# A transformer layer on 8 cores: earlier second half of the value weights, and the value bias on another engine

## The reference

```python
xn = layernorm(x)
q, k, v = split(xn @ W_attn + b_attn)            # 16 heads of 64
att = q k^T / 8 / temperature + slope_h * (kpos - qpos), causal
y = softmax(att) @ v @ W_proj + b_proj
g, u = xn @ wg^T / 127, xn @ wu^T / 127          # int32 weights, 3072 wide
out = x + y + (silu(g) * u) @ wd^T / 127
```

## Time and profile before

| | |
|---|---|
| Median of 3 runs | 975.07 us |
| The profiled execution | 976.52 us |
| its span, core 0 (the slowest) | 975.0 us |
| spans of cores 1 to 7 | 969.2, 968.2, 967.1, 970.6, 966.0, 964.9, 972.8 us |
| PE busy | 906.5 us (93%) |
| DVE, ACT, POOL busy | 500.9, 482.1, 285.3 us |
| Chain that ended last, by engine | PE 82%, DMA 6%, DVE 5%, issue 5%, ACT 2% |
| Mean DMA rate | 173 GB/s |

### The profile page before, as it was taken

One profiled execution on the slowest core, in us unless ns is written; L12 is line 12 of the kernel. 1 busy time (PEld: TensorE's weight loads), 2 busy tenths in 40 slices (PEclk: granted clock), 3 DMA queues, 4 the chain that ended last, 5 costly groups with the idle time before them and its releaser, 6 DMA issues.

```text
span 975.0 us, 19076 instructions; the slowest of 8 cores (964.9 to 975.0 us)
## 1 busy us (share of the span) xinstructions
PE 906.5 (93%) x6274; PEld 407.9 (42%) x6274; DVE 500.9 (51%) x1113; ACT 482.1 (49%) x583; POOL 285.3 (29%) x305
## 2 busy tenths in 40 slices
PE   2899899999999999999999999999983999999998
PEld 1445334444444444444444444444431444444443
DVE  4632377777777777777777777777210011110111
ACT  1545477776777767777767767766444000000000
POOL 2010123343333333233333333344470042412200
PEclk9999999999999999999999999999995999999999
DMA  8826089999999999999999999899579967342211
GB/s 186 197 71 109 9 163 202 230 213 209 164 204 206 221 208 194 196 203 197 198 214 206 184 188 198 185 207 213 119 186 186 240 189 257 128 176 85 87 44 44
DMA packets 334100, 168.56 MB, mean 173 GB/s; under 512 B 305459, under 2 KB 317748, under 8 KB 333108
## 3 DMA queue, kind: packets, MB, share of 16 engines
q1 hardware_dynamic: 325648, 136.88, 69.8%
q0 software_dynamic: 5328, 22.02, 11.4%
q10 hardware_dynamic: 3028, 8.44, 2.2%
HBM read 84.46 MB, written 20.97 MB: 108 GB/s over the span
## 4 chain that ended last, share of the span: by engine, by line
PE 82%; DMA 6%; DVE 5%; issue 5%; ACT 2%; DVEq 0%; ACTq 0%; SPq 0%
PE ps_gu L728 29%; PE ps_dn L847 17%; PE ps_m L708 10%; PE ps_s L792 8%; PE ps_y L805 6%; PE ps_dn L841 6%; PE ps_s L761 5%; DMA h_sc<-hst 3%; DMA xstage<-xin 2%; DVE sc L549 2%; DVE hst L492 1%; DMA bv_s<-battn_v 1%; ACT pr L665 1%; PE ps_y L708 1%; DVE st L502 0%
## 5 line engine op out<-in xcount | busy, mean ns | idle before, releaser
L665 ACT ACTIVATE pr<-sc,cm 128x2048 bf16<-128x2048 f32 (+15 forms) x256 | 291.0, 1198 | 60.0 <-DVE cm L549 59.9
L549 DVE CUSTOM_DVE_ANT_0 sc<-ps_s,ramp 128x1024 f32<-128x1024 f32 (+7 forms) x256 | 243.8, 988 | 74.6 <-PE ps_s L792 65.4
L728 PE MATMUL ps_gu<-xnT,wubuf 128*128 128x512 bf16 x768 | 206.0, 382 | 29.9 <-DVE hst L492 29.8
L728 PE MATMUL ps_gu<-xnT,wgbuf 128*128 128x512 bf16 x768 | 205.8, 382 | 6.1 <-ACT gh_s L619 6.1
L847 PE MATMUL ps_dn<-wdres,hb 128*128 128x512 bf16 x768 | 168.6, 380 | 0.0
L407 POOL TENSOR_SCALAR th_s<-th_s 128x512 f32<-128x512 f32 x96 | 59.4, 619 | 256.3 <-ACT th_s L617 256.1
L549 DVE CUSTOM_DVE_ANT_0 sc<-ps_s,ramp,cm 128x1024 f32<-128x1024 f32 (+7 forms) x128 | 100.0, 816 | 56.3 <-PE ps_s L792 55.4
L590 DVE SCALAR_TENSOR_TENSOR outsb<-ps_dn,xres 128x512 f32<-128x512 f32 x32 | 20.7, 687 | 200.8 <-PE ps_dn L847 149.6
L413 POOL TENSOR_TENSOR gs_s<-th_s,gh_s 128x512 bf16<-128x512 f32 x96 | 111.3, 1159 | 26.7 <-POOL th_s L407 25.9
L728 PEld LDWEIGHTS ps_gu<-xnT,wubuf 128*128 128x128 bf16 x768 | 66.8, 98 | 113.1 <-issue 54.5
L708 PE MATMUL ps_m<-xnT,wqk_b 128*128 128x512 bf16 x480 | 114.0, 380 | 0.0
(11 more groups left out here) (56 smaller groups left out, 455.7 us busy)
## 6 DMA issues: line engine op xcount, KB each, us to landing
h_sc<-hst SPq DMA_DIRECT2D x96, 128.0 KB, 3.2
hb<-h_sc SPq DMA_DIRECT2D x4, 3072.0 KB, 16.7
stg_i<-wg_r SPq DMA_DIRECT2D x20, 512.0 KB, 4.8
stg_i<-wu_r SPq DMA_DIRECT2D x20, 512.0 KB, 5.2
xstage<-xin SPq DMA_DIRECT2D x16, 512.0 KB, 6.8
xres<-xin POOLq DMA_DIRECT2D x16, 512.0 KB, 5.4
out<-outsb ACTq DMA_DIRECT2D x15, 512.0 KB, 2.7
stg_f<-wqk_r SPq DMA_DIRECT2D x12, 512.0 KB, 5.6
```

The costliest lines, as they stand in the source:

```text
L549: e.tensor_tensor_reduce(scores(n, g + (2 if b == 2 else 0), c0, w), ps_s[:, g * 1024:g * 1024 + w], ramp[:, T - wide + c0:T - wide + c0 + ...
L665: e.activation(pr[n % 3][:, b0 * 128:(b0 + blocks) * 128], scores(n, r, 0, blocks * 128), AF.Exp, bias=cm[:, at:at + 1], scale=-1.0).then_ ...
L728: mm = e.matmul(ps_gu[:, up * 512:up * 512 + 512], w[:, w0:w0 + 128], xnT[:, dc * T + tb * 512:dc * T + tb * 512 + 512], start=(dc == 0), ...
```

## The change

Two parts. In the start, POOL issues both halves of `wv_b` (and the Q and K weights between them) at once; the values of the second half are made up for at PE's i = 4 instead of 8, behind Q and K of the first 512 tokens, and from i = 5 on both halves are made for each tile. DVE's `evac_q` moves from its turns 7, 11, 15 to 6, 10, 14. In the rest, the value bias moves from ACT, after its last gate, to POOL: one pair each at batches k = 69, 93, ..., 189, two more behind `silu(90)`; and the 12 loads of down weights and the one of projection weights are issued together behind these two, no longer spread over six `silu`.

```diff
-        v_at = {i: [(i - 1, 0)] for i in range(1, 9)}
-        v_at[8] += [(tt, 1) for tt in range(4)]
-        for i in range(9, NT + 1):
+        v_at = {i: [(i - 1, 0)] for i in range(1, 5)}
+        v_at[4] += [(tt, 1) for tt in range(4)]
+        for i in range(5, NT + 1):
             v_at[i] = [(i - 1, 0), (i - 1, 1)]
-        v_at[9] += [(4, 1), (5, 1)]
-        v_at[10] += [(6, 1), (7, 1)]
...
 # gpsimd
-            e.dma_start(out=wv_b[:, 0:4096], in_=wv_r[0, :, :]).then_inc(sem["l_wv0"], 16)
-            cast_qk(0)
-            e.wait_ge(sem["l_const"], 16 * 5)
-            e.tensor_scalar(bv_s[:, :], bv_s[:, :], 127.0, None, AluOpType.mult).then_inc(sem["g_bv"], 1)
+            for half in range(2):
+                e.dma_start(out=wv_b[:, half * 4096:(half + 1) * 4096], in_=wv_r[half, :, :]).then_inc(
+                    sem[f"l_wv{half}"], 16)
+                if half == 0:
+                    cast_qk(0)
...
-            e.wait_ge(sem["v_xn"], 4)
-            e.dma_start(out=wv_b[:, 4096:8192], in_=wv_r[1, :, :]).then_inc(sem["l_wv1"], 16)
...
+            def value_bias(p):
+                e.wait_ge(sem[f"l_yt{p % 2}"], 16 * (p // 2 + 1))
+                if p == 0:
+                    ...   # bv_s times 127, once
+                e.tensor_scalar(VY[:, p * VS:p * VS + T], VY[:, p * VS:p * VS + T], bv_s[:, p:p + 1], None,
+                                AluOpType.add).then_inc(sem["g_y"], 1)
+            def late_weights():
+                ...       # the same waits as before
+                for j in range(HCP):
                     cast_down(j)
+                e.dma_start(out=wpj_b[:, :], in_=wproj_r[:, :]).then_inc(sem["l_wp"], 16)
             for k in range(NST):
                 for f in groups_ended(k, 0):
                     gate_and_loads(f)
+                if k % 24 == 21 and k >= 48:
+                    value_bias(k // 24 - 2)
             for f in range(NF_ATT + 1, NF):
                 gate_and_loads(f)
-                if NF_ATT + 2 <= f < NF_ATT + 2 + HCP // 2:
-                    late_weights(f - NF_ATT - 2)
+                if f == NF_ATT + 2:
+                    value_bias(NHP - 2)
+                    value_bias(NHP - 1)
+                    late_weights()
 # vector
-                if i >= 7 and i % 4 == 3:
+                if i >= 6 and i % 4 == 2:
                     evac_q(i // 4 - 1)
 # scalar
-            e.wait_ge(sem["g_bv"], 1)
-            for p in range(NHP):
-                e.wait_ge(sem[f"l_yt{p % 2}"], 16 * (p // 2 + 1))
-                e.activation(VY[:, p * VS:p * VS + T], VY[:, p * VS:p * VS + T], AF.Identity,
-                             bias=bv_s[:, p:p + 1]).then_inc(sem["a_y"], 1)
 # tensor
-                    if i == 8 and x == 1:
+                    if i == 4 and x == 1:
+                        ...   # Q and K of tokens 0 to 511, from behind the values of i = 4
                         e.wait_ge(sem["l_wv1"], 16)
...
-            e.wait_ge(sem["a_y"], NHP)
+            e.wait_ge(sem["g_y"], NHP)
```

More of the change, by code:

```diff
@@ L39 @@
     "l_hb0", "l_hb1", "l_yt0", "l_yt1", "l_xr0", "l_xr1", "l_xr2", "l_xr3", "s_out0", "s_out1",
-    "g_set", "g_w", "g_bv", "g_th", "g_s", "g_xr",
+    "g_set", "g_w", "g_bv", "g_y", "g_th", "g_s", "g_xr",
     "v_t", "v_cbq", "v_ln", "v_xn", "v_q", "v_mx", "v_rc", "v_y", "v_h", "v_out",
-    "a_c", "a_sd", "a_xe", "a_v", "a_k", "a_e", "a_th", "a_g", "a_y",
+    "a_c", "a_sd", "a_xe", "a_v", "a_k", "a_e", "a_th", "a_g",
     "p_c", "p_xT", "p_v", "p_qk", "p_s", "p_av", "p_g", "p_u", "p_d", "p_dl",
@@ L437, in cast_down @@
                     sem[f"l_wd{j // 2}"], 16)
[L439 to L449, removed]
+            def value_bias(p):
+                e.wait_ge(sem[f"l_yt{p % 2}"], 16 * (p // 2 + 1))
+                if p == 0:
+                    e.wait_ge(sem["l_const"], 16 * 5)
+                    e.tensor_scalar(bv_s[:, :], bv_s[:, :], 127.0, None, AluOpType.mult).then_inc(
+                        sem["g_bv"], 1)
+                    e.wait_ge(sem["g_bv"], 1)
+                e.tensor_scalar(VY[:, p * VS:p * VS + T], VY[:, p * VS:p * VS + T], bv_s[:, p:p + 1], None,
+                                AluOpType.add).then_inc(sem["g_y"], 1)
+            def late_weights():
+                e.wait_ge(sem["p_qk"], 8 * NHP)
+                e.wait_ge(sem["v_mx"], 2 * NSB)
+                e.wait_ge(sem["a_e"], 4 * NU)
+                for x in "abs":
+                    for i in range(3):
+                        e.wait_ge(sem[f"l_t{x}{i}"], 16 * ((NU - 1 - i) // 3 + 1))
+                for j in range(HCP):
                     cast_down(j)
-                if 2 * part + 2 == HCP:
-                    e.dma_start(out=wpj_b[:, :], in_=wproj_r[:, :]).then_inc(sem["l_wp"], 16)
+                e.dma_start(out=wpj_b[:, :], in_=wproj_r[:, :]).then_inc(sem["l_wp"], 16)
             for k in range(NST):
@@ L754, in _ @@
                         e.wait_ge(sem["l_wv0"], 16)
-                    if i == 8 and x == 1:
+                    if i == 4 and x == 1:
+                        e.wait_ge(sem["a_xe"], 4)
+                        e.wait_ge(sem["l_wq0"], 16)
+                        e.wait_ge(sem["a_c"], 1)
+                        q_or_k(0, 0, ps_m, range(DC)).then_inc(sem["p_qk"], 1)
+                        q_or_k(0, 1, ps_y, range(DC)).then_inc(sem["p_qk"], 1)
                         e.wait_ge(sem["l_wv1"], 16)
@@ L765, in _ @@
                     mm.then_inc(sem["p_v"], 1)
[L766 to L771, removed]
                 if i >= 9 and i % 4 == 1:
```

## The result

The changed kernel takes 985.77 us (median of 4 runs, 983.83 to 987.71), the kernel before 974.97 (4 runs, 973.22 to 976.52): a ratio of 1.0116, 95% interval 1.0097 to 1.0135. It is slower by 10.8 us, where I had forecast 978.0 and a range up to 982.0. The sign was right, the size was not.

A forecast was written before the change was run, and what follows sets the result against it. PE, 82% of the chain, was taken as the bound, so only its idle or slow-clock places counted. 976.5 - 3.4 + 5.0 + 0.5 - 0.7 = 977.9, taken as 978.0 us; range 973.5 to 982.0.

The forecast's parts named there:

- Tile loads that now share engines with it (tile 7) are wanted later than before: At the start, claimed that tile loads sharing DMA engines with the early wv_b half are wanted later; no cost was added.
- Until 36.17 us PE has done the same work: At the start, claimed PE's work is the same in both kernels up to 36.17 us.
- 0.6 us, while POOL has nothing else due: At the start, issuing wv_b's second half sooner costs POOL one issue of 0.6 us, with nothing else due there.
- The wait for `wv_b` behind K: At 36.17 us PE waits for wv_b's second half behind Q and K: +0.8 us, bounds 0 and 2.9.
- The gain of 3.4 for PE's order: At the start: tile 7's wait goes (-2.7), core 0's clock fall goes (-1.5), a wv_b wait comes (+0.8): -3.4 us.
- evac_q: One turn earlier, DVE normalises tiles 10 and 14 late and PE idles: 2 x 2.5 = +5.0 us, bounds 0 and 8.0.
- the rival: The clock falls behind both evac_q waits, at tiles 10 and 14: +3.0 us, 981.0 in all; chance 0.11.
- The bias pass: Value bias on POOL during attention: 2.3 us per 128x2048 pass, costing +0.5 us, bounds 0 and 6 x 2.5.
- The cover by 19.44 us: At the gates' end, 12 us of POOL work before silu(91) is swallowed by PE's 19.44 us idle: cost 0.
- The loads together (-0.7): Down weights 4.6 us later let group 91's store land sooner before the projection: -0.7 us, bounds -4.9 and +2.8.
- The port lock: Rival: in attention, each of six POOL bias passes holds DVE up for 2.3 us, 984.9 in all; chance 0.04.
- the start's first term: Second half of wv_b queued early with catch-up at i = 4: a net gain, -3.4 us.

The follow-up runs named there:

- se_catchup: Kernel before with only PE's new order at the start (catch-up at i = 4, two values per tile from i = 5): 973.90 us, ratio 0.9995.
- wv_early: Kernel before with only the second half of wv_b issued early, right behind the Q and K weights: 976.08 us, ratio 1.0010.
- s_evac_back: Kernel before with all edits of the start except evac_q, which stays in DVE's turns 7, 11, 15: 979.46 us, ratio 1.0046.
- v_only: Kernel before with the start unchanged and only the rest changed (value bias on POOL, 13 late weight loads together): 974.88 us, ratio 1.0005.
- two_op: Changed kernel with POOL's value bias pass written as two operations, add the bias and multiply by 1.0: 985.75 us, ratio 1.0121 to the kernel before.
- se_iota_late: Kernel before with PE's new order and wv_b's second half queued at once; evac_q and the ramp as before: 974.91 us, ratio 1.0018.

## Why the prediction was wrong

By its own sum, the start was to cost -3.4 + 5.0 = +1.6 us. It costs 10.5 at the start of attention: PE's order -0.7, the two edits beside the first tiles +5.0, evac_q +6.1.

- **"Tile loads that now share engines with it (tile 7) are wanted later than before": this step failed.** I looked at tile 7 and not at tiles 4 and 5, the next ones due. Tile 5's statistics stand before tile 4's normalising in DVE's order, and tile 4 is what PE needs ahead of Q and K. "Until 36.17 us PE has done the same work" was wrong with it: PE comes to tile 4's transpose at 30.55 on core 0 before, and at 35.52 in the changed kernel, having waited 3.84 us for it.
- **A moved wait was not priced at all.** The edit took POOL's wait for the constants away from in front of the ramp. I costed the issue that came in ("0.6 us, while POOL has nothing else due") and not the iota that now runs while DVE normalises tile 0. The two failures make each other worse: at the start of attention 0.7 and 1.5 us alone, 5.0 together; in the mean span 2.7, 1.2 and 5.9.
- **The wait for `wv_b` behind K: right as a place, hidden by the failure.** Predicted 0.8 (0 to 2.9). In the changed kernel there is none: the half lands at 10.43 + 23.9 = 34.3 us and PE comes to it at 42.4. Where PE comes in time and the load is issued late it is 1.1 in the mean and 2.7 at most (se_catchup). The gain of 3.4 for PE's order was 0.7: the 2.7 for tile 7 and the 1.5 of clock were core 0's, the slowest, and over the eight cores the wait for tile 7 was 0 to 2.66 us, 1.2 in the mean, with a fall behind it on core 0 alone.
- **evac_q: mechanism, place and sign right, size 6.1 for 5.0.** Two idles of 2.00 us each against 2.15 foreseen, ended by DVE's xn_st as foreseen. What is missing is the fall of the clock behind one of the two (1.7 us), which stood in the rival and in the bounds (up to 8.0), not in the value. Comparing 2.15 with a 2.06 behind which the clock held was a poor guide: behind 2.00 us it fell at one of the two tiles and held at the other, and it also held behind 2.50 (wv_early, core 1) and 2.87 (s_evac_back, core 1).
- **The bias pass: 5.45 us for 2.3, and no cost.** I took it from casts and a two-operation pass; neither row has one operation. The term of +0.5 was 0.
- **The cover by 19.44 us held**, though silu(91) started 17.7 us behind the end of silu(90) and not 12: PE idled 13.51 us before up group 92 and 1.01 before 95. **The loads together (-0.7)** measured nothing, v_only is at 1.0005; beside the start with `evac_q` back, loads and value bias cost 3.4 us, by a cause that stays open. The wait for `wpj_b` came (0.5 to 4.7 us, some with a clock fall); from the last score to the projection it is 107.0 us in the mean of the changed kernel's cores, 105.5 in two_op and 105.6 before.
- **The port lock** had 0.04 as a rival in attention, and there it did nothing: 687 ns before and after. What looks like it came where I hadn't looked, in the start: on all 64 cores of the eight kernels with the ramp early, xn_st ends 0.55 us behind the end of the iota. The Trainium skill ("SBUF — State Buffer", SBUF: two separate sides) has whichever of a VectorE operation in a two-port mode and a GpSimd operation starts second wait for the whole of the first. The length of the wait agrees with this; the order does not everywhere, as in the changed kernel xn_st starts 0.51 us before the iota (10.45 and 10.96) and yet waits. Whether xn_st runs in such a mode no run here shows.

The range ended at 982.0 because every one of its cases took the start's first term as a gain. No rival had the queued megabyte delay the tiles.

## What to carry to other kernels

When a bulk load is issued earlier, price the next small loads that it will meet, from the first one that anybody waits for, and not only the one whose wait it is meant to end. When a wait is moved on an in-order engine, write down what now runs sooner behind its old place, and beside which instructions of the other engines. Delays that hardly show singly can reach a clock fall together, so test two suspects in all four combinations. And look at the mean over the cores beside the time: here the slowest core hid 2 us of one edit.

## What the hardware showed that I had not expected

- On POOL a tensor_scalar with one operation takes 2.4 to 2.8 times as long as one with two: 1.50 us against 0.62 for 128x512 (bf16 or f32, immediate or per-partition operand, add or multiply; a two-operation f32 one is the 619 ns of the earlier trace rows), and 5.45 against 1.98 us for 128x2048 in bf16. Multiplying by 1.0 in addition is the faster form.
- DVE's normalising pass, 128x1024 from f32 to bf16, took 0.81 us alone and 1.8 to 2.95 beside POOL's iota and affine_select, in each kernel with the ramp ahead of the constants. It ends 0.55 us behind the iota's end on each of their 64 cores, though the iota reads nothing from SBUF.
- A 1 MB load with conversion took 23.9 us to land when it was queued behind two others at 10 us, beside the tile loads, and 12.5 when issued by itself at 26.6 (core 0, changed kernel and before). With it queued, the statistics of tile 5, whose 0.5 MB load ran in that time, began 3.5 us later in the mean (28.6 in se_iota_late for 25.1 in se_catchup).
